# First group of x loaded in two parts, and the places of an inverse's Newton steps rearranged, in an audio tower on one core

## What is computed

```
xp = x.reshape(8, 64, 5, 200)                     # 5 patches of 200 samples: 320 positions a batch
fr = rfft(xp); feats = concat(abs(fr), angle(fr)) # 2 * 101 features
h  = gelu(feats @ W1 + b1) @ W2 + b2              # 202 -> 808 -> 128
# state space layer on layernorm(h):
A_bar = (I + dt/2 A) @ inv(I - dt/2 A)            # 32 x 32
B_bar = dt * inv(I - dt/2 A) @ B
state = tanh(state @ A_bar.T + u_t @ B_bar.T)     # 320 steps, one after another
h = h + (states @ C.T + u * D) @ W_out.T + b_out
# gated recurrent layer on layernorm(h): 320 steps, 256 hidden units
h = h + sigmoid(gru(layernorm(h)) @ Wo.T + bo)
```

## Time and profile before

| | us |
|---|---|
| median of 3 runs | 890.94 |
| lowest and highest | 890.02 to 891.04 |
| profiled execution | 889.93 |
| its span, from the first to the last instruction | 888.1 |

### The profile page before, as it was taken

One profiled execution on the slowest core, in us unless ns is written; L12 is line 12 of the kernel. 1 busy time (PEld: TensorE's weight loads), 2 busy tenths in 40 slices (PEclk: granted clock), 3 DMA queues, 4 the chain that ended last, 5 costly groups with the idle time before them and its releaser, 6 DMA issues.

```text
span 888.1 us, 40652 instructions
## 1 busy us (share of the span) xinstructions
PE 831.7 (94%) x17111; PEld 704.6 (79%) x17111; DVE 583.0 (66%) x3495; ACT 370.9 (42%) x2016; POOL 74.5 (8%) x189
## 2 busy tenths in 40 slices
PE   8999999989999999999999999999999998988875
PEld 7677667778888888888888888888888887877765
DVE  5343538376777776767767777777677777676655
ACT  5565766433343443433434434334334343343322
POOL 3111102110000000100000001000000000000000
PEclk9979999955555555555555555555555555555555
DMA  7100000000000000000000000000000000000000
GB/s 172 38 1 0 1 1 1 2 3 3 7 3 6 7 3 6 7 3 6 4 6 7 3 6 7 3 6 4 7 6 4 6 7 3 6 6 3 7 3 8
DMA packets 7454, 8.53 MB, mean 10 GB/s; under 512 B 1343, under 2 KB 6557, under 8 KB 7271
## 3 DMA queue, kind: packets, MB, share of 16 engines
q1 hardware_dynamic: 6965, 5.92, 2.9%
q0 software_dynamic: 256, 0.01, 0.0%
q10 hardware_dynamic: 50, 0.00, 0.0%
HBM read 4.62 MB, written 1.31 MB: 7 GB/s over the span
## 4 chain that ended last, share of the span: by engine, by line
PE 85%; ACT 7%; DVE 4%; issue 3%; POOL 0%; POOLq 0%; DVEq 0%
PE ps L1527 42%; PE ps L1533 11%; PE ps L1340 8%; PE ps L1238 4%; PE ps L1440 3%; PE ps L1541 3%; PE ps L1404 3%; DVE h_hi L479 2%; PE ps L1448 2%; ACT addend L847 1%; PE ps L1322 1%; PE ps L1329 1%; PE ps L1310 1%; PE ps L1260 1%; PE ps L1254 1%
## 5 line engine op out<-in xcount | busy, mean ns | idle before, releaser
L1527 PE MATMUL ps<-h_hi,w_first 128*128 128x8 f16 x2552 | 267.6, 170 | 27.8 <-DVE h_hi L479 27.7
L1527 PEld LDWEIGHTS ps<-h_hi,w_first 128*128 128x128 f16 x2552 | 220.3, 104 | 89.8 <-DVE h_hi L479 89.8
L1527 PE MATMUL ps<-h_hi,w_rest 128*128 128x8 f16 x5104 | 275.8, 168 | 0.0
L1527 PEld LDWEIGHTS ps<-h_hi,w_rest 128*128 128x128 bf16 x5104 | 241.0, 105 | 0.1
L837 ACT ACTIVATE tanh_r<-ps 128x16 f32<-128x16 f32 x320 | 59.2, 185 | 250.2 <-PE ps L1533 249.7
L1533 PE MATMUL ps<-h_lo,w_first 128*128 128x8 f16 x2560 | 159.0, 168 | 0.1
L1527 PE MATMUL ps<-rh_hi,w_first 128*128 128x8 f16 x1276 | 136.0, 172 | 12.6 <-DVE rh_hi L1132 0.9
L1527 PEld LDWEIGHTS ps<-rh_hi,w_first 128*128 128x128 f16 x1276 | 109.0, 104 | 39.6 <-DVE rh_hi L1132 1.1
L1527 PE MATMUL ps<-rh_hi,w_rest 128*128 128x8 f16 x2552 | 138.6, 168 | 0.0
L479 DVE TENSOR_TENSOR_SCAN h_hi<-coef,addend 128x32 f16<-128x32 f32 x320 | 73.3, 229 | 83.7 <-ACT addend L847 83.7
L1527 PEld LDWEIGHTS ps<-rh_hi,w_rest 128*128 128x128 bf16 x2552 | 121.2, 105 | 0.0
(11 more groups left out here) (210 smaller groups left out, 1375.3 us busy)
## 6 DMA issues: line engine op xcount, KB each, us to landing
x_sb<-in_x SPq DMA_DIRECT2D x4, 500.0 KB
out<-res SPq DMA_DIRECT2D x20, 64.0 KB, 2.0
W_sb<-in_L_tok_W SPq DMA_DIRECT2D x1, 606.0 KB
W_sb<-in_L_tok_W SPq DMA_DIRECT2D x1, 384.0 KB
wnat<-in_L_ffn_Wwr SPq DMA_DIRECT2D x1, 256.0 KB, 5.5
wnat<-in_L_ffn_Wwz SPq DMA_DIRECT2D x1, 256.0 KB, 11.8
wnat<-in_L_ffn_Ww SPq DMA_DIRECT2D x1, 256.0 KB, 10.4
wunat<-in_L_ffn_Wur SPq DMA_DIRECT2D x1, 128.0 KB, 7.1
```

Source lines behind the costliest of these rows:

```text
L1527: mm(gate(c, j, g, m), w[:, m * 128:(m + 1) * 128], state[:, k * NB:(k + 1) * NB], start=False, stop=False, skip_group_check=True)
```

## The change

- The x of group 0 is loaded by two DMAs, the first with patches 0 to 2 (600 of the 1000 samples of a row), the second with patches 3 and 4, each with a semaphore of its own. Both are issued by SP ahead of the tables. DVE's `even_odd` of group 0 is done in two calls, one for each part, each of three instructions and each with a wait for its own part. The transposes of group 0 wait for their own part, in place of one wait for all.
- WARM goes from 52 to 36.
- EARLY goes from 8 to 6: halves 6 and 7, and the three runs of `busy` that stood around them (12, 6 and 6 transposes), are no longer in the opening. Half 6 gets place (0,0,1), with the wait for `im_read` that stood ahead of it, and half 7 place (0,0,2).
- `blocked` also names (0,0,0) and (1,0,0), and frees (1,5,1), (1,6,1), (3,5,1) and (3,6,1). Counted out, halves 8 to 27 move three places in n = 0; in n = 2 each place holds the half two lower than before; the last half, 79, keeps place (4,4,0).

```diff
--- before.py
+++ after.py
@@ -34,9 +34,9 @@
 TINY_POWER = 1e-34
 EPS = 1e-5
 NEWTON = 40
-WARM = 52
+WARM = 36
 BUSY = 6
-EARLY = 8
+EARLY = 6
 
 XT_PIECE, SKIP_PIECE = 4, 6
 SQRT_PIECE, ATAN_PIECE = 4, 2
@@ -252,6 +252,7 @@
 
 
         x_in = [sem(f"x_in{g}") for g in range(NP)]
+        x_rest = sem("x_rest")
         dft_in = sem("dft_in")
         parts_done = [sem(f"parts_done{g}") for g in range(NP)]
         w1_in = sem("w1_in")
@@ -415,13 +416,13 @@
         HALVES = 2 * NEWTON
 
         def blocked(n, m, slot):
-            if slot == 1 and n % 2:
+            if slot == 1 and n % 2 and (n > 3 or m < MC - 2):
                 return True
             if n in (2, 4) and slot and m in (XT_PIECE, SKIP_PIECE):
                 return True
             if n in (2, 4) and (m, slot) == (SQRT_PIECE + 2, 0):
                 return True
-            if (n, m, slot) in ((0, SQRT_PIECE + 2, 1), (2, SQRT_PIECE + 1, 1), (4, SQRT_PIECE + 1, 1)):
+            if (n, m, slot) in ((0, 0, 0), (1, 0, 0), (0, SQRT_PIECE + 2, 1), (2, SQRT_PIECE + 1, 1), (4, SQRT_PIECE + 1, 1)):
                 return True
             return n in (1, 3, 5) and (m, slot) in ((ATAN_PIECE + 1, 2), (ATAN_PIECE + 2, 0))
 
@@ -467,12 +468,13 @@
             s0, s1, cols = patches(h)
             return tile[:, 0:cols.stop - cols.start].rearrange("p (s b c) -> p s b c", b=NB, c=CP)
 
-        def even_odd(eng, ops, g):
-            xs = x_sb[:, g, :].rearrange("p (s n) -> p s n", s=NS)
-            eng.wait_ge(x_in[g], 16)
-            ops.tensor_copy(even[:, g, :, 0:KP + 1:KP], xs[:, :, 0:KP + 1:KP])
-            ops.tensor_tensor(even[:, g, :, 1:KP], xs[:, :, 1:KP], xs[:, :, 2 * KP - 1:KP:-1], ALU.add)
-            return ops.tensor_tensor(odd[:, g], xs[:, :, 1:KP], xs[:, :, 2 * KP - 1:KP:-1],
+        def even_odd(eng, ops, g, part=None):
+            s0, s1 = (0, NS) if part is None else ((0, S0), (S0, NS))[part]
+            xs = x_sb[:, g, :].rearrange("p (s n) -> p s n", s=NS)[:, s0:s1]
+            eng.wait_ge(x_rest if part else x_in[g], 16)
+            ops.tensor_copy(even[:, g, s0:s1, 0:KP + 1:KP], xs[:, :, 0:KP + 1:KP])
+            ops.tensor_tensor(even[:, g, s0:s1, 1:KP], xs[:, :, 1:KP], xs[:, :, 2 * KP - 1:KP:-1], ALU.add)
+            return ops.tensor_tensor(odd[:, g, s0:s1], xs[:, :, 1:KP], xs[:, :, 2 * KP - 1:KP:-1],
                                      ALU.subtract).then_inc(parts_done[g], 1)
 
         def scan(v, dst):
@@ -488,7 +490,8 @@
             def load(g):
                 sp.dma_start(x_sb[:, g, :], x[:, CP * g:CP * (g + 1), :]).then_inc(x_in[g], 16)
 
-            load(0)
+            sp.dma_start(x_sb[:, 0, 0:S0 * PATCH], x[:, 0:CP, 0:S0 * PATCH]).then_inc(x_in[0], 16)
+            sp.dma_start(x_sb[:, 0, S0 * PATCH:], x[:, 0:CP, S0 * PATCH:]).then_inc(x_rest, 16)
             sp.dma_start(cos_sb[0:KP], dft[:, 0, 0, :]).then_inc(dft_in, 16)
             sp.dma_start(cos_sb[KP:KP + 1], dft[0:1, 1, 0, :]).then_inc(dft_in, 16)
             sp.dma_start(sin_sb[:], dft[1:KP, 0, 1, :]).then_inc(dft_in, 16)
@@ -712,8 +715,6 @@
             newton(5)
             act.wait_ge(bias_psum, 1)
             a.activation(biasT[:], bank(6)[:, 0:32], ACT.Copy).then_inc(su_act, 1)
-            for i in range(6, EARLY):
-                newton(i)
 
             def ssm_tanh(c, k):
                 act.wait_ge(s_psum, CH * c + k + 1)
@@ -934,7 +935,8 @@
                     scalar=0x7fffffff, in1=half_of(imag[:, g, :], h).bitcast(U32),
                     op0=ALU.bitwise_and, op1=ALU.bitwise_or).then_inc(ang_done, 1)
 
-            even_odd(dve, v, 0)
+            even_odd(dve, v, 0, 0)
+            even_odd(dve, v, 0, 1)
             dve.wait_ge(su_act, 1)
             v.tensor_scalar(dtrow[:], dtrow[:], 1e-4, 1.0, ALU.max, ALU.min).then_inc(su_dve, 1)
             dve.wait_ge(su_dve, 1)
@@ -1206,8 +1208,8 @@
             mm, tr = nc.tensor.matmul, nc.tensor.transpose
             def transposes(g, h):
                 s0, s1, cols = patches(h)
-                if h == 0:
-                    pe.wait_ge(parts_done[g], 1)
+                if h == 0 or g == 0:
+                    pe.wait_ge(parts_done[g], h + 1)
                 if 2 * g + h > 1:
                     pe.wait_ge(patT0_copied, 2 * g + h)
                     pe.wait_ge(patT1_copied, 2 * g + h)
@@ -1293,12 +1295,6 @@
             pe.wait_ge(rows_in, 16 * 8)
             pe.wait_ge(re_read, 2)
             tr(bank(6)[:, 0:32], bias_rows[:], ident[0:32, 0:32]).then_inc(bias_psum, 1)
-            for i in range(6, EARLY):
-                if i == 6:
-                    pe.wait_ge(im_read, 2)
-                busy(2 * BUSY if i == 6 else BUSY, 7)
-                newton(i)
-            busy(BUSY, 7)
             pe.wait_ge(w1_in, 32)
             pe.wait_ge(mag_done, 1)
             pe.wait_ge(su_act, 3)
@@ -1372,6 +1368,8 @@
             def serial(n, m, slot):
                 if (n, m, slot) in SLOTS:
                     i = SLOTS[n, m, slot]
+                    if (n, m, slot) == (0, 0, 1):
+                        pe.wait_ge(im_read, 2)
                     if n % 2 and (n, m, slot) == min(key for key in SLOTS if key[0] == n):
                         pe.wait_ge(re_read, min(n + 3, 2 * NP))
                     if n and n % 2 == 0 and (m, slot) == (0, 0):
```

## The result

| | before | after |
|---|---|---|
| median of 5 runs | 890.99 | 885.85 |
| lowest and highest | 890.02 to 892.71 | 883.96 to 887.07 |
| profiled execution | 889.93 | 883.96 |
| its span | 888.1 | 882.1 |

After / before is 0.9939, 95% interval 0.9925 to 0.9952. So the change gains 5 to 6 us, where I had forecast 9.8.

What follows compares the result with a forecast made beforehand. PE bounds the stage ahead of the recurrence, for part of n=1 through its clock. Terms 3.1 + 1.1 + 2.2 + 4.4 - 1.0 = 9.8 us took the median from 890.94 to 881.1; range 879.0 to 888.0.

Steps and rivals of the forecast that it cites:

- named first among the rivals: Ahead of the recurrence: the old low clock stretch of n=1 stays, 886.2 us; chance 0.17 shared with a new fall.
- its twin: Ahead of the recurrence: another low clock stretch as long comes, costing 6.5 us, 887.6; shares the chance of 0.17.
- the sum: All five terms, 9.8 us gained, 881.1 on the median; with bounds 879.0 to 884.7, chance 0.66.
- End of the opening: Opening, W1 matmuls: without halves 6 and 7 and their fillers the first angle half starts 3.1 us earlier.
- start: Start of the opening: fewer warm-up transposes and x in two loads gain 1.1 us, bounds 0 to 1.6.
- The late split: First x loads: queue costs by row, so the second part lands near 10.8 us; 884.3 us, chance 0.07.
- The stall at the head of n=1: Head of n=1: without place (1,0,0) PE's stall shrinks to near 0.5 us idle, gaining 2.2 us.
- The clock in n=1: n=1 from its second piece: granted clock 1.00 as in n=3, 14.71 us in place of 19.12, gaining 4.4.
- Four new places: Newton halves at (1,5,1), (1,6,1), (3,5,1), (3,6,1): cost 0.25 us each, 1.0 in all, bounds 0.6 to 2.8.
- The slower one: Opening gap before the first angle half: clock falls and stays low through n=0, 16.8 us more, 897.9; chance 0.07.

Runs made afterwards that it cites:

- before_rows: Kernel before with only the last down product of each token group contracted over all 128 rows (added rows zero); median 884.37 us, ratio 0.9955.
- full_rows: Changed kernel with the last down product of each token group contracted over 128 rows in place of 40 (added rows zero); median 880.94 us, ratio 0.9904.
- fill_head: Changed kernel with six identity transposes on PE in the idle time at the head of n=1; median 885.81 us, ratio 0.9953.
- one_load: Changed kernel with the first group of x in one load and one folding call again, WARM still 36; median 884.89 us, ratio 0.9934.
- places_alone: Kernel before with only the new Newton places and EARLY at 6, one x load and WARM at 52; median 886.12 us, ratio 0.9948.
- four_out: Changed kernel with 128-row last down products and six transposes at n=1's head, minus the last four Newton halves and the four new places; 878.35 us, one run.
- after_again: The changed kernel itself, unedited, in five further runs with a second profile; median 884.39 us, ratio 0.9938 to the kernel before.
- all_fills: Changed kernel with 128-row last down products, six identity transposes at the head of n=1 and six in the opening; median 881.39 us, ratio 0.9896.
- all_warm30: The kernel all_fills with 30 warm-up transposes in place of 36; median 880.92 us, ratio 0.9889 to the kernel before.

## Why the prediction was right or wrong

**The direction and the range were right, the forecast was not.** I had 881.1; the kernel takes 884.4 to 885.9. The case that happened is the one that I named first among the rivals and gave 0.17 together with its twin: the low stretch of n=1 stays, 886.2. That the range holds the result is due to this rival, and not to the sum, whose own bounds end at 884.7.

**End of the opening and start, 3.1 + 1.1: right.** The first angle half starts at 25.05; I had 25.3. The warm-up ends at 7.85 (I had 8.2), and DVE turns to x of group 1 at 11.88 (12.1), with the wait for the DMA that I expected. What I had not expected is why: both parts of x land before the single load did, at 5.46 and 6.65 against 7.51; I had put the second at 7.5 to 8.3. DVE was therefore done with both parts at about 7.3, and it was PE's warm-up that set the copies. The late split is refuted. The Trainium skill, page "DMA: Bandwidth & Descriptors", section "Anatomy of one DMA — SWDGE (gpsimd) path", gives a DMA a fixed 2.0 us. That section is on DMAs that GpSimd issues, and these are issued by SP; that the second part would pay the 2.0 us after the first, and land at 9.5, was my reading. The trace has 1.19 us between the parts, so it does not agree with that reading.

**The stall at the head of n=1, 2.2: right.** The gain grows from 4.17 to 6.40 over the head, and 0.54 us of idle time is left where I had "near 0.5". (Of the two table loads that I counted into the old stall only the second, from 50.71, lies in it; the first ended at 49.77, while PE still worked.)

**The clock in n=1, 4.4: this is the step that failed.** Pieces 1 to 6 of n=1 took 19.41 us; with the 0.70 that the two new places cost there taken off, 18.71, against 19.12 before: 0.4 us of 4.4. The sentence "With 0.5 us left at the head, I expect 1.00 in n=1 as well" rested on n=3, where 1.13 us of idle time did no harm. What the runs showed in its place: the clock fell in n=1 in both traces of the changed kernel, for 10.24 us, behind 0.54 and 0.53 us of idle time. The comparison with n=3 took a stall for harmless because a longer one was; the rows beside them had a difference in plain sight, 40 rows at the one and 128 rows at the other. before_rows and full_rows suggest that it counts: with only the product changed, an idle time of 1.48 us left a low stretch of 3.42 us in place of 13.65, and one of 0.54 us left none, in the traced runs. By the estimate all ten runs of the changed kernel had 718 us or more at the low level. Of the 31 runs with the full product, in seven kernels, five had that much (885.15, 888.53, 888.83, 884.69 and 887.49), and 19 had under 716. So the full product goes with fewer long falls. A cause is not shown by that. fill_head, without idle time but with the thin product, held the clock once in five, and one_load and places_alone held it in n=1 in at least five runs of thirteen, with both conditions in place. A rival was not tested: the moment. The same 36 warm-up transposes took 5.54 to 7.07 us in the traces, so the same work comes at another time after the start in each execution, and every edit moves it too. What decides in a single execution stays open.

The term was also too large in itself. With the clock held, pieces 1 to 6 take 6.57 + 9.47 = 16.04 us in full_rows, 15.33 without the places, so 3.8 us were to be had and not 4.4. n=1 is not as fast as n=3: from a half of W1 on magnitudes to the one on angles it takes 0.90 us in n=1 and 0.71 in n=3, at the same clock. The changed kernel, in n=1 and then in n=3:

```profile
62.44 0.65 PE L1240 MATMUL ps<-magT,W_sb 101*128 101x256 f32 x2
63.09 0.41 PE L1256 MATMUL ps<-Xn,step_w 128*128 128x32 f32 x2
63.34 0.68 PE L1240 MATMUL ps<-angT,W_sb 101*128 101x256 f32 x2
```

```profile
93.55 0.68 PE L1240 MATMUL ps<-magT,W_sb 101*128 101x256 f32 x2
94.06 0.36 PE L1258 MATMUL ps<-DY 128*128 128x64 f32 x2
94.26 0.43 PE L1240 MATMUL ps<-angT,W_sb 101*128 101x256 f32 x1
```

In n=1 an even Newton half stands between them, in n=3 an odd one. An even half waits for two copies of ACT and an odd one for one; that this is the reason is not shown.

**Four new places, -1.0: mis-sized, 1.4.** From before to after, pieces 4 to 6 grew by 0.70 in n=1 and 0.73 in n=3, and four_out gives the same 0.36 us for each place. The half took its whole 0.36 us, where I had let a third of it vanish under its neighbours. PE is busy at these places, so there was nothing for it to vanish under.

**The rivals.** The slower one has happened at its place, in one_load, for 6.82 us and not for the whole of n=0; its mechanism was real and its price, 16.8 for some 3 us, far too high, because I let the low level last to the end of n=0 against the evidence that I had cited myself, that n=1's ended by itself. That the fall of n=1 stayed is why the changed kernel's gain is smaller than the sum; the kernels in which falls are rare gain 9.9 to 10.4. That this is near the 9.8 of the sum is in part luck: some 1.5 us of it are the shorter product on 128 rows, which the sum did not have.

## What to carry to other kernels

When the granted clock falls after a stall, look at what PE does on either side of it and not only at how long it idles: here a product with a contraction over 40 rows stood there, and padding it to 128 with zeros cost nothing, went with rarer long falls and gained, by itself, as much as the whole change. Before a stage is counted at the full clock, look for every other place with waits and short bursts, and fill those too, since the fall may come there next. And time a kernel in several executions: one with a fall in some of its runs shows two groups of times, and one trace shows one of them. Look then for the runs that go against the theory: here the trace of one_load had both conditions and no fall.

## What the runs showed of the hardware that was not expected

*Around products on 40 rows PE paused, 0.1 us on the way in and 0.1 on the way out.* Six matmuls of the down product in n=3, with no idle time of PE around them, first with 40 rows (changed kernel), then with 128 (full_rows). PEld is the load of the weights, which can run ahead of the matmul:

```profile
92.44 0.74 PEld L1402 LDWEIGHTS ps<-W_sb,hid 40*128 40x128 f32 x6 [0.33 <-issue]
92.44 0.93 PE L1402 MATMUL ps<-W_sb,hid 40*128 40x128 f32 x6
93.30 0.30 PEld L1256 LDWEIGHTS ps<-Xn,step_w 128*128 128x128 f32 x2
93.30 0.41 PE L1256 MATMUL ps<-Xn,step_w 128*128 128x32 f32 x2
```

```profile
87.36 0.85 PEld L1405 LDWEIGHTS ps<-W_sb,hid 128*128 128x128 f32 x6
87.58 0.83 PE L1405 MATMUL ps<-W_sb,hid 128*128 128x128 f32 x6
88.14 0.30 PEld L1259 LDWEIGHTS ps<-Xn,step_w 128*128 128x128 f32 x2
88.25 0.31 PE L1259 MATMUL ps<-Xn,step_w 128*128 128x32 f32 x2
```

The next instruction starts 0.86 us after the first matmul at 40 rows and 0.67 at 128. The matmuls themselves are not slower: inside the six they start 0.11 us apart in both traces. The difference lies at the ends. At 128 rows the first weight load starts 0.22 us ahead of its matmul and that of the next instruction 0.11 ahead; at 40 rows neither starts before its matmul does. From the first matmul at 40 rows to the second, and from the last one to the next at 128, it takes 0.2 us each in place of 0.11. Between products on 128 and on 101 rows the traces show no such pause (0.11 us). So padding is no even exchange, as I had it for full_rows, but a gain of 0.2 us a group: from n=2 to the last piece of n=6 the trace of full_rows is 1.3 us shorter than that of the changed kernel (92.33 and 93.64). Whether it is the idle rows or these two pauses that count for the clock, no run tells.

*Two loads landed sooner than one.* 300 KB landed at 5.46 us and the other 200 KB at 6.65, where the 500 KB of the single load landed at 7.51, though the first issue starts at 0.73 us in both. The other traces agree: 6.10 to 6.66 for the second of two, 7.43 to 7.79 for the single one. Why is open. DVE came to x of group 1 earlier for it, and found it not yet there in some executions: it waited 0.36 us in the changed kernel, 1.33 with a shorter warm-up, and not at all in after_again. Whether that load landed later than before, no row says.

*The clock differs between executions of one kernel.* The warm-up's 36 transposes took 6.36 us in the changed kernel's trace and 7.00 in that of all_fills. The Trainium skill, page "TensorE: Matmul & The Clock Gate", Part 4, says that the full clock doesn't engage for transposes, of TensorE's transpose mode. The traces list these as MATMUL and don't tell the mode. For them it does not hold: in the changed kernel PE had done nothing but transposes when their number rose from 7 between 5 and 6 us to 12 between 7 and 8, and six of them take 0.87 us in its opening (15.94), at 1.00, and 1.49 in that of all_warm30 (16.18), at 0.50.
